# Graph network on one core: the dense part behind the third layer done group by group inside that layer, and its end and the self products inside the fourth

## What is computed (the reference, cut)

```python
x = _layernorm(x + _L0_gnn_ref(...))        # attention over the edges
x = _layernorm(x + _L1_gnn_ref(...))        # relu((x + sum over edges) @ W)
x = _layernorm(x + _L2_gnn_ref(...))        # third layer
x = _layernorm(x + _L3_gnn_ref(...))        # fourth layer

# third layer
e_w = sigmoid(silu(edge_attr @ edge_W1 + edge_b1) @ edge_W2 + edge_b2)
x_agg = silu(x[src] @ agg_W + agg_b) * e_w
out = segment_sum(x_agg, dst) / maximum(cnt, 1)
h = silu(concat([x, out]) @ upd_W1 + upd_b1) @ upd_W2 + upd_b2 + x @ res_W
return (h - mean) * rsqrt(var + 1e-5) * ln_g + ln_b

# fourth layer
msg = (x[src] + rel_emb[edge_type]) @ W_msg.T + b_msg
return x @ W_self.T + b_self + segment_sum(msg, dst) / maximum(deg, 1)
```

## Time and profile before

| | us |
|---|---|
| median of 3 runs | 1138.64 |
| lowest and highest | 1137.24, 1138.89 |
| the profiled execution, its own time | 1142.04 |
| its span in the trace | 1140.0 |
| its mean granted TensorE clock | 0.948 of full |

### The profile page before, as it was taken

How to read it: one execution, slowest core, us unless ns; L and a number is a source line. 1 busy time by engine, 2 the same in 40 slices (tenths; PEclk the granted TensorE clock), 3 DMA queues, 4 the chain that set the end, 5 groups by cost and what they waited for, 6 DMA issues and landing times.

```text
span 1140.0 us, 28055 instructions
## 1 busy us (share of the span) xinstructions
PE 1010.5 (89%) x10463; PEld 876.6 (77%) x10463; DVE 913.9 (80%) x2141; ACT 700.8 (61%) x1507; POOL 221.8 (19%) x267
## 2 busy tenths in 40 slices
PE   4798979799999999968999998799999999818994
PEld 3343557699999999966777776689999999716784
DVE  6776999889899998988888898877677777697445
ACT  3466856454555555559889885777665565453663
POOL 4403040000000000000000001057676677130000
PEclk9897999899999999988999999799999999959997
DMA  6000020444444444304333334245454554224872
GB/s 152 1 1 1 4 65 5 138 148 141 152 152 152 153 149 152 122 2 147 117 119 122 115 102 125 58 139 136 139 139 139 145 141 108 81 74 137 251 219 57
DMA packets 79130, 128.23 MB, mean 112 GB/s; under 512 B 11083, under 2 KB 53142, under 8 KB 78764
## 3 DMA queue, kind: packets, MB, share of 16 engines
q1 hardware_dynamic: 73513, 115.20, 32.7%
q0 software_dynamic: 5056, 10.36, 3.9%
q10 hardware_dynamic: 426, 0.85, 0.3%
HBM read 101.50 MB, written 24.88 MB: 111 GB/s over the span
## 4 chain that ended last, share of the span: by engine, by line
PE 75%; DVE 13%; ACT 5%; DMA 3%; issue 3%; POOL 0%; POOLq 0%; SPq 0%; DVEq 0%; ACTq 0%
PE PS L2038 14%; PE PS L2227 13%; PE PS L2026 11%; PE PS L2210 7%; PE PS L2266 6%; PE PS L2143 6%; PE PS L2111 3%; PE PS L2118 2%; PE PS L1864 2%; ACT X L1064 2%; PE PS L1877 2%; PE PS L1941 2%; DMA adj_d<-ring 2%; DVE st L1617 1%; DVE vo L1387 1%
## 5 line engine op out<-in xcount | busy, mean ns | idle before, releaser
L988 ACT CAST vo<-XT 128x768 f32<-128x768 bf16 (+1 forms) x218 | 180.6, 829 | 158.2 <-PE PS L2227 84.0
L820 POOL DMA_INDIRECT XT<-tab,ring x158 | 156.9, 993 | 109.2 <-PE PS L2227 55.9
L2038 PE MATMUL PS<-vo 128*128 128x133 f32 x1300 | 175.9, 284 | 1.0 <-DVE vo L1489 1.0
L2038 PEld LDWEIGHTS PS<-vo 128*128 128x128 f32 x1300 | 157.2, 191 | 1.1 <-issue 1.1
L2026 PE MATMUL PS<-kp,ring 128*128 128x132 bf16 x1950 | 146.4, 221 | 3.2 <-DVE ring L1357 1.7
L2227 PE MATMUL PS<-vo 128*128 128x128 f32 x984 | 133.4, 280 | 1.8 <-DVE vo L1756 1.8
L2026 PEld LDWEIGHTS PS<-kp,ring 128*128 128x128 bf16 x1950 | 125.4, 97 | 5.4 <-DVE ring L1357 1.8
L1125 ACT CAST ring<-PS 128x512 bf16<-128x512 f32 (+1 forms) x175 | 118.1, 687 | 10.4 <-DMA adj_d<-ring 10.4
L2227 PEld LDWEIGHTS PS<-vo 128*128 128x128 f32 x984 | 118.5, 191 | 1.9 <-ACT vo L988 1.9
L1122 ACT CAST adjf_r<-PS 128x512 fp32r<-128x512 f32 (+1 forms) x175 | 117.0, 679 | 4.1 <-PE PS L2111 4.0
L1365 DVE TENSOR_TENSOR XT<-iotab,XT 128x768 bf16<-128x768 bf16 (+1 forms) x218 | 119.5, 549 | 0.0
(11 more groups left out here) (328 smaller groups left out, 2101.7 us busy)
## 6 DMA issues: line engine op xcount, KB each, us to landing
ring<-rows_d SPq DMA_DIRECT2D x146, 416.0 KB, 4.7
adj_d<-ring SPq DMA_DIRECT2D x100, 128.0 KB, 1.7
adj_d<-ring SPq DMA_DIRECT2D x75, 96.0 KB, 1.7
ring<-adj_d SPq DMA_DIRECT2D x11, 640.0 KB, 4.2
vo<-adj_d SPq DMA_DIRECT2D x9, 640.0 KB, 5.3
vo<-adj_d SPq DMA_DIRECT2D x8, 480.0 KB, 4.6
ring<-adj_d SPq DMA_DIRECT2D x7, 480.0 KB, 4.6
XT<-tab,ring POOLq DMA_INDIRECT x158
```

The lines of the kernel that those rows point to most:

```text
L820: G.indirect_dma_start(far_rows[:, f % FBUF, :], None, tab[2], bass.IndirectOffsetOnAxis(ap=far_row[:, t:t + 1], axis=0)).then_inc(far_in[ ...
L988: C.copy(ohd[:, k % 3, 0:n, :], ohb[:, k % 3, 0:n, :]).then_inc(hots_wide, 1)
L2038: T.matmul(bank(6 + b % 2)[:, 0:VW], ohd[:, k % 3, i, :], vals[:, k % 3, i, :], start=j == 0, stop=j == JN - 1).then_inc(scattered, 1)
```

## The change

Seven groups of the dense part are taken apart. With the sizes of this case LATE is 5, CUT is 20, and `at(x)` is x.

- Groups 0 to 4 are done inside the loop over the third layer's batches. Group i has its first product at batch `up_at(i)` (23, 41, 57, 75, 93), its second four batches later, and its two normalisations in the 13 batches after that, one small piece of work behind each batch. The products go to the PSUM bank that an odd batch leaves free. TensorE waits for that bank to be read before it gathers three batches later.
- The shift `ln_b` is added to X group by group in batches 3 to 9, not in one instruction ahead of the loop. The gain is multiplied in on VectorE, no longer on GpSimd.
- Group 5's first product comes ahead of the last scatter. The rest of groups 5 and 6 (blocks 20 to 24, normalised as one unit of five) is spread over the first 40 steps of the fourth layer. These steps are reordered: source blocks 0 to 19 for range 0, then for range 1, and only then blocks 20 to 24 of both.
- Transposes, their copies and self products are done group by group from step 52 on, one group every eight steps, in banks 4 and 5. VectorE adds `bias3`, X and the self bias per group in the same steps.
- The loads of adjacency chunks follow the new order of the steps, and chunk 0 no longer waits for the end of the gathers.
- Conditional code for the other form of input (`redo`, some 150 VectorE instructions, jumped over here) comes in at step 42 on three engines, and shorter blocks ahead of the third layer's loop.

```diff
+    LATE = BANKS - 2
+    CUT = 4 * LATE // ACH * ACH
+    STEPS = [(0, b) for b in range(CUT)] + [(1, b) for b in range(CUT)]
+    STEPS += [(0, b) for b in range(CUT, NB)] + [(1, b) for b in range(CUT, NB)]
+    STEPS += [(q, b) for q in range(2, BANKS) for b in range(NB)]
+    CHUNKS = []
+    for q, b in STEPS:
+        if (q, b // ACH) not in CHUNKS:
+            CHUNKS.append((q, b // ACH))
+    last_step = {(q, b // ACH): s for s, (q, b) in enumerate(STEPS)}
+    sum_end = {q: s for s, (q, b) in enumerate(STEPS) if b == NB - 1}
+    REDO = 2 * CUT + 2
...
+    def at(x):
+        return x * 2 * CUT // 40
+
+    def self_from(i):
+        return 2 * NB + 2 + 8 * i
+
+    def ends(i):
+        return (JN * (blocks(i)[-1] + 1) - 1) // BT
+
+    def up_at(i):
+        return (ends(i) + 6) | 1
+
+    def up2_at(i):
+        return up_at(i) + 4
...
+    LAST_ODD = max(k for k in range(NBATCH - 1) if k % 2 and k >= 3 and len(batch(k)) == BT)
...
+    def odd_bank(k):
+        return 2 * (k % 3) + 1
+
+    def unit(i):
+        return min(i, LATE)
+
+    def unit_nodes(u):
+        return slice(4 * u, 4 * u + 4 if u < LATE else NB)
...
-            sp.wait_ge(gathered_up, NT + near_until(NT))
-            sp.wait_ge(far_ready, len(far_tiles))
-            for q in range(BANKS):
...
+            sp.wait_ge(hots_src, 3 * NU)
+            for n, (q, i) in enumerate(CHUNKS):
...
+                if n == RBUF * HW // (ACH * 4 * P):
+                    sp.wait_ge(far_ready, len(far_tiles))
+                if n == 2 * RBUF * HW // (ACH * 4 * P):
+                    sp.wait_ge(gathered_up, NT + near_until(NT))
+                if n == 3:
+                    sp.wait_ge(scattered, 2 * NT)
+                    sp.wait_ge(ag_ready, 2 * BANKS)
...
+                if n >= CBUF:
+                    widened(sp, last_step[CHUNKS[n - CBUF]])
...
-                norm_wait(pool, 3, piece_of(i))
-                G.tensor_tensor(T1[:, nodes(i), :], T1[:, nodes(i), :],
-                                lng[:, :].unsqueeze(1).to_broadcast([P, len(blocks(i)), F]), ALU.mult).then_inc(g_done, 1)
...
+            def update_step(i, k):
+                if k == up_at(i) + 1:
+                    silu_hidden(i)
+                for turn, start in enumerate((up2_at(i), up2_at(i) + 8)):
+                    if k == start + 3:
+                        unit_deviation(i, turn)
+                    if k == start + 5:
+                        unit_rows(i, turn)
...
-            for i in range(BANKS):
-                act.wait_ge(up1_sum, i + 1)
-                C.activation(T1f[:, cols(i)], T1f[:, cols(i)], ACT.Silu).then_inc(up1_act, 1)
-            normalise(3, T1)
-            normalise(4, X)
-            for i in range(BANKS):
-                round_rows(4, i)
-            copy_xt(2)
+            for k in range(NBATCH, up2_at(LATE - 1) + 14):
+                for i in range(LATE):
+                    update_step(i, k)
+            silu_hidden(LATE)
...
+                for i in range(2, LATE):
+                    if s == 4 * i - 6:
+                        round_last(i)
+                if s == at(3):
+                    silu_hidden(BANKS - 1)
+                if s == at(12):
+                    unit_deviation(LATE, 0)
+                if s == at(15):
+                    unit_rows(LATE, 0)
+                if s == at(27):
+                    unit_deviation(LATE, 1)
+                if s == at(30):
+                    unit_rows(LATE, 1)
+                if s == at(34):
+                    round_last(LATE)
+                    round_last(BANKS - 1)
+                for i in range(BANKS):
+                    if s == self_from(i) + 2:
+                        copy_last(i)
...
-            loose(V.tensor_tensor(X[:, :, :], X[:, :, :], lnb[:, :].unsqueeze(1).to_broadcast([P, NB, F]), ALU.add))
...
+            def update_step(i, k):
+                if k == up_at(i):
+                    hidden_sum(i, odd_bank(k))
+                k -= up2_at(i)
+                if k == 0:
+                    add_update(i, odd_bank(up2_at(i)))
+                elif k == 1:
+                    dve.wait_ge(update_added, i + 1)
+                    mark[i] = unit_stats(nodes(i))
+                elif k == 2:
+                    unit_variance(i, mark[i])
+                elif k == 4:
+                    unit_scale(i, 0)
+                elif k == 7:
+                    mark[i] = unit_gain(i)
+                elif k == 8:
+                    mark[i] = unit_add(i, mark[i])
+                elif k == 9:
+                    dve.wait_ge(dve_order, mark[i])
+                    mark[i] = unit_stats(nodes(i))
+                elif k == 10:
+                    unit_variance(i, mark[i])
+                elif k == 12:
+                    unit_scale(i, 1)
...
+                if 3 <= k < 3 + BANKS:
+                    mark["x", k - 3] = shifted(k - 3)
+                for i in range(LATE):
+                    update_step(i, k)
+            for k in range(NBATCH, up2_at(LATE - 1) + 13):
+                for i in range(LATE):
+                    update_step(i, k)
+            hidden_sum(LATE, odd_bank(LAST_ODD))
...
+            def late_step(s):
+                if s == at(2):
+                    hidden_sum(BANKS - 1, odd_bank(LAST_ODD))
+                if s == at(4):
+                    add_update(LATE, odd_bank(LAST_ODD - 2))
+                if s == at(6):
+                    dve.wait_ge(update_added, LATE + 1)
+                    unit_stats(nodes(LATE))
+                if s == at(8):
+                    add_update(BANKS - 1, odd_bank(LAST_ODD - 2))
+                if s == at(9):
+                    dve.wait_ge(update_added, BANKS)
+                    mark[LATE] = unit_stats(nodes(BANKS - 1))
+                if s == at(11):
+                    unit_variance(LATE, mark[LATE])
+                if s == at(14):
+                    unit_scale(LATE, 0)
+                if s == at(19):
+                    mark[LATE] = unit_gain(LATE)
+                if s == at(21):
+                    mark[LATE] = unit_add(LATE, mark[LATE])
+                if s == at(23):
+                    dve.wait_ge(dve_order, mark[LATE])
+                    mark[LATE] = unit_stats(unit_nodes(LATE))
+                if s == at(26):
+                    unit_variance(LATE, mark[LATE])
+                if s == at(29):
+                    unit_scale(LATE, 1)
+                if s == at(36):
+                    remainder(LATE)
+                    remainder(BANKS - 1)
...
+            def self_step(i, s):
+                if s == self_from(i):
+                    dve.wait_ge(bias3_step, 1)
+                    rows_wait(dve, LATE, 1)
+                    mark[i] = loose(V.tensor_tensor(NX[:, nodes(i), :], bias3[:, nodes(i), :], X[:, nodes(i), :], ALU.add))
+                if s == self_from(i) + 3:
+                    dve.wait_ge(dve_order, mark[i])
+                    mark[i] = loose(V.tensor_tensor(NX[:, nodes(i), :], NX[:, nodes(i), :], bself[:, :].unsqueeze(1).to_broadcast([P, len(blocks(i)), F]), ALU.add))
+                if s == self_from(i) + 6:
+                    dve.wait_ge(dve_order, mark[i])
+                    dve.wait_ge(xr, BANKS + i + 1)
+                    V.tensor_tensor(NX[:, nodes(i), :], bank(5)[:, 0:width(i)].rearrange("p (b f) -> p b f", f=F), NX[:, nodes(i), :], ALU.add).then_inc(xr_add, 1)
...
+                    if k == up_at(i) + 3:
+                        pe.wait_ge(up1_sum, i + 1)
+                    if k == up2_at(i) + 3:
+                        pe.wait_ge(update_added, i + 1)
...
+            def hidden(i, n):
+                pe.wait_ge(ag_ready, 1 * BANKS + i + 1)
+                T.matmul(bank(n)[:, 0:width(i)], Wu1[:, 1, :], AG[:, cols(i)], start=True, stop=True).then_inc(up1, 1)
+
+            def update(i, n):
+                pe.wait_ge(up1_act, i + 1)
+                for d, b in enumerate(blocks(i)):
+                    o = T.matmul(bank(n)[:, d * P:(d + 1) * P], T1f[:, b * P:(b + 1) * P], Wu2[:, :], start=True, stop=True)
+                o.then_inc(up2, 1)
+
             gather2(0)
             gather2(1)
             for k in range(NBATCH):
                 if k + 2 < NBATCH:
                     gather2(k + 2)
+                for i in range(LATE):
+                    if k + 2 == up_at(i):
+                        hidden(i, odd_bank(k + 2))
+                    if k + 2 == up2_at(i):
+                        update(i, odd_bank(k + 2))
+                if k == NBATCH - 1:
+                    pe.wait_ge(update_added, LATE)
+                    hidden(LATE, odd_bank(LAST_ODD))
                 scatter2(k)
             with pe.If(general == 1):
...
-            x_transposed(2)
-            dense(xr, lambda i: xt_wait(pe, 2, i), [(XT, WsT[:, :])])
-            pe.wait_ge(xr_add, 2 * BANKS)
-            pe.wait_ge(xp_rest, 3 * BANKS)
-            for q in range(BANKS):
...
+            def x_turned(i):
```

(82 more changed lines are left out.)

238 lines of the change are left out of this document (159 added, 79 removed).

## The result

The changed kernel takes 1113.91 us in the median of four runs, against 1138.77 us of the kernel before on the same chip. The ratio of the two is 0.9752 (95% interval 0.9726 to 0.9778). In the median is one run of 2451.68 us, which the ratio leaves out; without it the median is 1113.17. Forecast were 1116.9 us, 1107 to 1130. The profiled execution took 1114.64 us with a span of 1112.8.

The account below looks back on a forecast made before the run. TensorE bounds the loop and fourth layer; the dense part between is a VectorE and ScalarE chain. Terms -1.8 + 12.3 - 49.0 + 7.3 + 1.0 + 8.5 = -21.7 us, from 1138.64 to 1116.9 us; range 1107 to 1130.

Parts of the forecast that it names:

- Start of the loop: Ahead of the third layer's loop: without the one-piece shift the chain is shorter until ScalarE's copy limits it, -1.8 us.
- Loop: Third layer's loop: +9.8 us for TensorE's added products, 1.0 for batches 3 to 9, 1.5 for other stalls; +12.3 us.
- Table changes: ScalarE: 9 switches in the loop and 2 behind it, 1.28 us each without drain; 11.5 us in the loop, under cover.
- Rival 3: ScalarE's table switches behind the loop have a drain the trace doesn't show: +2.6 us, 1119.5 us; chance 0.05.
- Border: Last scatter to first step: 52.1 us shrink to 3.1, -49.0 us.
- Steps 0 to 39: Fourth layer's first 40 steps: late work makes them fall behind, 26.2 us instead of 18.9, +7.3 us.
- Clock: Start of the fourth layer's steps: TensorE's 3.1 us pause may halve its clock for some 4 us, +1.0 us.
- Steps 40 to 174: Rest of the fourth layer: stall of 3.3 us goes, self products and transposes +8.7, adds 2.1, jump 1.0; +8.5 us.
- Rival 1: Hand-offs overlap better: ScalarE alone sets steps 0 to 39, no stalls in loop, none from clock or jump: 1107.5 us; chance 0.20.
- Rival 2: Fourth layer's first 40 steps: the late chain is serial, 34 us, +7.8 us, 1124.7 us; chance 0.14.
- Rival 4: Third layer's loop: VectorE's small instructions hold up TensorE, 39.4 us come on, 1153.8 us, slower than before; chance 0.04.
- rival 5: Early groups don't finish in the loop; group 4's second norm, about 5 us, is left behind it: 1122 us; chance 0.04.

Follow-up runs that it names:

- run 1: Changed kernel with the shift ln_b added in one instruction ahead of the loop again: 1115.22 us, loop 241.74 us.
- run 11: Changed kernel with the first product of groups 0 to 4 computed twice, on a third chip: 1116.61 us, loop 244.41 against 240.12 us.
- run 12: Changed kernel with two more VectorE statistics instructions behind each of batches 23 to 105, 166 in all: 1113.33 us, loop 240.12 us.
- run 2: Changed kernel with identity instead of Silu, so ten of eleven table loads are gone: 1110.05 us, loop 240.07 us, steps 97.24 us.
- run 3: Changed kernel without the conditional code at step 42 on TensorE, ScalarE and VectorE: 1115.06 us, steps 97.66 against 97.84 us.
- run 7: Changed kernel without transposes, their copies, self products and the adds of them, on another, slower chip: 1123.32 us, steps 85.75 us.
- run 4: Changed kernel with the fourth layer's steps in plain order, late pieces at half their step numbers: 1120.51 us, steps 102.41 us.
- run 5: Changed kernel with the first product of groups 0 to 4 computed twice, on another, slower chip: 1137.85 us, loop 266.04 us.
- run 6: Changed kernel with 166 more VectorE statistics instructions in the loop, on another, slower chip: 1138.44 us, loop 264.33 us.
- run 9: The changed kernel itself, unedited, run six times on a third chip: 1111.57 us, 0.9742 of the kernel before, loop 240.12 us.
- Run 8: Changed kernel with self adds one step later, steps 14, 16, 32 widened by VectorE, group 5's Silu after rounding and step 0's widening: 1104.25 us.

## Why the prediction was right, and where it was off

**The sum was 5.4 us short of the gain** between the two spans, and the time 3.0 us too long by the medians; inside the range. That the medians come nearer is luck: the forecast put the gain too low, and by the medians the gain is 2.3 us smaller than by the spans. The mechanism was the right one; the terms that were mis-sized are the stalls in the loop and in steps 0 to 39, and the clock, all put too high. By steps:

- **Start of the loop:** right (1.8), and undoing it costs 2.0 (run 1). That the next late thing was the one named, ScalarE's copy, is shown by the wait of 1.5 us for it in the profile after.
- **Loop:** the 9.8 us for TensorE's added products were right to 0.1, and run 11 shows the rule behind them. What failed are the two terms beside them, 1.0 us for batches 3 to 9 and 1.5 for all other stalls: both measured 0. I had put VectorE at 84% and taken stalls for likely. It is at 80%: the new pieces add up to 38.6 us in a view of groups, near the 39.4 that I had, but they overlap in part, and the busy time grew by 30.7. Run 12 shows that 92% brings no stall either. Three buffers and hand-offs two batches ahead absorb every piece.
- **Table changes:** I costed them by the row, a load of 1.28 us with nothing behind it, and the profile after says the same: the load ends at 990.35 and Silu starts at 990.37. The Trainium skill (ScalarE: Activation LUTs, section What ACT_TABLE_LOAD costs) gives 1283 ns for the load, which this case shows to the nanosecond, and a drain of 1380 ns beside it, which it does not show. Rival 3 (+2.6) falls by run 2, where ten of the loads together were worth 0.6.
- **Border:** right (3.1 forecast, 2.63 measured). The surplus is mostly that the sum of group 5 starts 0.4 us ahead of the last scatter's end, not behind it, and ends 0.3 behind it where I had 0.6.
- **Steps 0 to 39:** my walk gave 26.2 us, and they take 24.4. The places were right in kind: the largest pauses are those behind the rows, at steps 16 and 32 (1.31 and 0.83), and there is 0.27 at step 5. But the walk had added pauses at 25 and 34, for statistics and rounding, that did not come. This term was too large by 1.8. I had called all three engines full; over the first 25.3 us TensorE is busy 22.66, ScalarE 20.55 and VectorE 17.45.
- **Clock:** 1.0 us forecast, 0 in this execution. In three of twelve profiled executions with such a pause it came, at 1.5 us; see the last section.
- **Steps 40 to 174:** 8.5 and 8.7, in part by luck: two errors cancel. The jump was to cost 1.0 and costs at most 0.2 (run 3). The adds ahead of widenings were put at 0.3 each, 2.1 in all. There are five pauses, of 0.35 each, but moving the adds gave 3.5 us: 1.8 of idle time, and 1.6 by which TensorE's busy time falls too, for a reason that no run shows. Taken from the 12.1 us of the self part (run 7), that leaves 8.6 for its products and transposes, which I had at 8.7.

**The rivals.** Rival 1 (1107.5) is right in three of its parts: no stalls in the loop, none from the clock in this profile, none from the jump. Its main part, that ScalarE alone sets steps 0 to 39, is wrong: 21.3 us by that, 24.4 measured. By the spans the gain lies between it and the forecast; by the medians the time does too, nearer to the forecast. Rival 2 (a serial late chain, 34 us) is wrong here. The late chain does need its cover: with half of it the steps lose 4.6 us (run 4). Rival 4 falls by run 12 and rival 5 by the border.

## What to carry to other kernels

In this kernel, work that was moved under an engine which is busy all the time cost what it takes on that engine, within 0.2 us of ten, and nothing on the others, up to the 92% that was tried: don't add a surcharge for "84% busy" if each has its buffers ahead. What does cost is the place in a queue. A piece of 0.7 to 2 us, in front of a small conversion that the bounding engine takes next, can stall it (five of the seven adds did, and both sets of rows); move it by one step, or give the conversion to the other engine.

## What the runs showed of the hardware that I had not expected

**The same pause cost the clock in some executions and not in others.** Twelve of the profiled executions have the pause of 2.6 us (in one 3.4) on TensorE between the two stages. In nine the granted clock stayed at 1.00. In three (runs 5, 6 and 11) it went to 0.50 for 3.4 us, beginning 0.2 us before TensorE took up work again (run 5) or 0.6 and 0.7 us after it. Run 11, the pause and then 2.5 us of the steps:

```profile
990.44:993.08 2.64, 0.00 (x1) 0.03 (x1) 1.64 (x4) 2.62 (x6) 0.00 (x0) 1.00 0.90 303
994.00:996.50 2.50, 2.50 (x10) 2.11 (x9) 1.23 (x3) 1.44 (x4) 0.00 (x0) 0.50 1.02 422
```

The same places of run 9, with the same pause:

```profile
988.73:991.36 2.63, 0.00 (x0) 0.03 (x1) 1.62 (x4) 2.61 (x6) 0.00 (x0) 1.00 0.92 286
992.28:994.78 2.50, 2.50 (x17) 2.06 (x15) 1.85 (x5) 1.86 (x4) 0.00 (x0) 1.00 1.02 414
```

In 2.5 us TensorE starts 10 instructions in one and 17 in the other. The steps take 99.39 and 97.85 us, so the fall costs 1.5. Run 8, with its pause of 1.18 us, kept its clock. What decides it was not found. It need not be chance: runs 5 and 11 are the same kernel and fell both times, the changed kernel kept its clock both times (the profile after and run 9), and the kernel of runs 6 and 12 fell behind the pause of 3.4 us and not behind 2.6. No kernel was seen both ways behind the same pause.

**A chip on which TensorE paused with nothing to wait for.** In runs 5 to 7 TensorE paused in the loop without waiting for any engine or load that the profile shows. The waits of TensorE in the loop of run 6 (in us in total, times, longest):

```profile
PE PS L2500 <- issue: 6.8, 18, 1.1
PE PS L2517 <- issue: 4.4, 11, 0.9
```

The same view of run 9's loop has no row. TensorE is busy in run 6 252.2 of 264.3 us, so its busy time is 12 us longer too, with single pieces as long as ever (the scatter's matmul 280 ns against 279). Some of it is the clock: behind the first pauses it is 0.50 for 6.8 us in runs 5 and 6 and for 3.4 in run 7, which at half speed is 3.4 and 1.7 us. The pauses come in the same places: all three runs have them 2.7, 4.1, 5.6, 7.0 and 8.4 us behind the first scatter. Since run 7 has no edit there and the kernel before was 3% slower too, it is the chip or its state and not a kernel. The cause stays open. The packets of the instruction queue take no longer there: 0.6% of the DMA engines' time in the loop of run 6, 0.7% in that of run 12, the same kernel.
